# Mamba stage: the output rows' norm statistics from ScalarE sums instead of VectorE bn_stats

## The reference, cut to what matters

```python
x = x + mamba(layernorm(x), ...)      # 16 batches, one after the other
x = x + moe(layernorm(x), ...)        # all 8192 tokens: needs every batch's norm and gate scores
x = x + attention(layernorm(x), ...)
x = x + moe(layernorm(x), ...)

def layernorm(x, eps=1e-05):
    m = mean(x); v = var(x)           # over the 256 channels of a token
    return (x - m) / sqrt(v + eps)
```

## Time and profile before

| what | us |
|---|---|
| median of 3 runs | 3346.77 (3342.35 to 3348.41) |
| span of the profiled execution, first to last instruction | 3323.2 |
| own time of the profiled execution | not given on the page; its span is 23.6 below the median |
| Mamba stage in the profile, start to the last score copy | about 1813 |
| busy over the span: TensorE, VectorE, GpSimd, ScalarE | 2699.6, 2305.5, 2124.3, 1719.1 |

### The profile page before, as it was taken

One profiled execution on the slowest core, in us unless ns is written; L12 is line 12 of the kernel. 1 busy time (PEld: TensorE's weight loads), 2 busy tenths in 40 slices (PEclk: granted clock), 3 DMA queues, 4 the chain that ended last, 5 costly groups with the idle time before them and its releaser, 6 DMA issues.

```text
span 3323.2 us, 54121 instructions
## 1 busy us (share of the span) xinstructions
PE 2699.6 (81%) x20202; PEld 1494.4 (45%) x20202; DVE 2305.5 (69%) x2483; ACT 1719.1 (52%) x3115; POOL 2124.3 (64%) x1317
## 2 busy tenths in 40 slices
PE   5787788877888788887864299996999999269998
PEld 2233333433333334333332156664676777235665
DVE  1799999999999999999996632211666676542211
ACT  3677777777777777777763022222444443022222
POOL 1899999999999999999994035533333333024543
PEclk9899999988998889988976599998999999579999
DMA  3556556665566565665561124432111111213442
GB/s 112 106 128 148 140 140 135 152 142 134 122 147 153 140 141 136 141 147 141 132 130 65 22 58 90 90 58 56 40 46 53 53 46 40 67 34 83 90 90 26
DMA packets 227392, 330.02 MB, mean 99 GB/s; under 512 B 40545, under 2 KB 116833, under 8 KB 227010
## 3 DMA queue, kind: packets, MB, share of 16 engines
q1 hardware_dynamic: 202562, 292.49, 35.8%
q0 software_dynamic: 24576, 34.10, 6.1%
HBM read 240.52 MB, written 85.98 MB: 98 GB/s over the span
## 4 chain that ended last, share of the span: by engine, by line
PE 44%; POOL 25%; DVE 20%; issue 7%; ACT 3%; DMA 2%; SPq 0%; DVEq 0%; POOLq 0%; ACTq 0%
POOL m_side L584 15%; PE t_wb L2062 8%; POOL m_hc L593 7%; DVE m_pair L668 7%; PE f_h L1341 6%; PE g_h L1341 6%; DVE m_hc L668 5%; PE m_wk L771 3%; PE f_yp L1355 3%; PE g_yp L1355 3%; PE t_num L2062 2%; DVE m_hc L677 2%; PE t_a_ps L2062 2%; PE m_y L863 2%; PE m_pair L919 2%
## 5 line engine op out<-in xcount | busy, mean ns | idle before, releaser
L584 POOL TENSOR_TENSOR m_side<-m_du_r,m_bc 128x1024 f32<-128x1024 f32 x416 | 975.0, 2368 | 13.2 <-DMA m_du_r<-ddd 13.0
L351 ACT ACTIVATE m_pair<-m_delta_r,m_a_neg 128x512 f32<-128x512 f32 x832 | 539.7, 681 | 179.1 <-DVE m_hc L677 128.7
L593 POOL TENSOR_TENSOR m_hc<-m_hc,m_bc 128x1024 f32<-128x1024 f32 x208 | 492.3, 2370 | 99.4 <-DVE m_hc L668 97.7
L668 DVE TENSOR_TENSOR_SCAN m_pair<-m_pair,m_side 128x1024 f32<-128x1024 f32 x240 | 548.0, 2283 | 3.3 <-ACT m_pair L351 2.8
L863 PE MATMUL m_y<-m_hc,m_fold 128*32 128x512 f32 x2048 | 322.1, 703 | 229.4 <-DVE m_hc L677 120.9
L668 DVE TENSOR_TENSOR_SCAN m_hc<-m_pair,m_side 128x1024 f32<-128x1024 f32 x176 | 397.8, 2275 | 28.5 <-ACT m_pair L351 28.5
L677 DVE TENSOR_TENSOR m_hc<-m_pair,m_bc 128x1024 f32<-128x1024 f32 x304 | 370.5, 1219 | 7.3
L771 PE MATMUL m_wk<-m_xnT,m_w_in 128*128 128x512 f32 x512 | 276.1, 666 | 10.7 <-DVE m_cw_diag L725 9.8
L771 PE MATMUL m_wk<-m_xs,m_cw_diag 128*128 128x512 f32 x512 | 244.1, 605 | 15.5 <-ACT m_xs L416 15.5
L919 PE MATMUL m_pair<-m_b_diag,m_du_t 128*32 128x128 f32 x6144 | 203.6, 289 | 44.0 <-DVE m_hc L668 24.4
L919 PEld LDWEIGHTS m_pair<-m_b_diag,m_du_t 128*32 128x32 f32 x6144 | 178.8, 117 | 125.1 <-issue 123.7
(11 more groups left out here) (308 smaller groups left out, 4884.8 us busy)
## 6 DMA issues: line engine op xcount, KB each, us to landing
m_delta_r<-ddd SPq DMA_DIRECT2D x256, 256.0 KB, 6.8
m_du_r<-ddd SPq DMA_DIRECT2D x256, 256.0 KB, 7.7
m_bc<-bcd SPq DMA_DIRECT2D x256, 128.0 KB, 3.0
ddd<-m_delta SPq DMA_DIRECT2D x32, 512.0 KB, 3.2
ddd<-m_du SPq DMA_DIRECT2D x32, 512.0 KB, 4.2
f_w<-in_w SPq DMA_DIRECT2D x24, 512.0 KB, 6.2
g_w<-in_w SPq DMA_DIRECT2D x24, 512.0 KB, 6.1
m_xt<-in_x SPq DMA_DIRECT2D x16, 512.0 KB, 10.7
```

Source lines behind the costliest of these rows:

```text
L351: last = nc.scalar.activation(to, delta_r[:, c % 2, q, :], ACT.Exp, scale=a_neg[:, c * NQ + q, st:st + 1])
L584: nc.gpsimd.tensor_tensor(side[:, un % RING, :, :], du_r[:, c % 2, 2 * h:2 * h + 2, :], bc[:, 0, st:st + 1, :].to_broadcast([P, 2, T]), AL ...
L593: nc.gpsimd.tensor_tensor(hc[:, un % RING, :, :], hc[:, un % RING, :, :], bc[:, 1, st:st + 1, :].to_broadcast([P, 2, T]), ALU.mult).then_i ...
L668: nc.vector.tensor_tensor_scan(to, decay, added, 0.0, ALU.mult, ALU.add).then_inc(S["scan"], 1)
```

## The change

VectorE's bn_stats and bn_aggr of the output rows are taken out. ScalarE instead makes two passes over them with an accumulated output: the sum of each row (`out_sums`, function Identity, in units 9 and 12), from it the negated mean (`out_mean`, unit 12), then the sum of the squares of the rows less their mean (`out_squares`, function Square, units 14 and 18). What the passes write besides goes into the tile of the normed rows and is overwritten later. GpSimd's `out_stats` has three operations in place of four and moves from unit 17 to unit 20, the norm `out_norm3` moves from units 20 and 22 to 22 and 23. In the epilogue the same steps follow one another.

```diff
--- before.py
+++ after.py
@@ -171,8 +171,9 @@
 
         xr = s.sb("xr", [P, TJ, C])
         x1t = xr
-        stat1 = s.sb("stat1", [P, TJ, 6])
-        mv1 = s.sb("mv1", [P, TJ, 2])
+        sum1 = s.sb("sum1", [P, TJ])
+        nmean1 = s.sb("nmean1", [P, TJ])
+        sq1 = s.sb("sq1", [P, TJ])
         ve1 = s.sb("ve1", [P, TJ])
         rstd1 = s.sb("rstd1", [P, TJ])
         nm1 = s.sb("nm1", [P, TJ])
@@ -191,7 +192,7 @@
                  "a_exp aneg const one halo diag "
                  "bs agg ve rstd nm xn tr trev ix ixev cv cvev u iz izev sz xp xdev dt "
                  "ab ex sp de du dz "
-                 "btr b_t dut du_t dg0 dg1 dA dBu dBp scan hD hP sum yg op x1 bs1 agg1 ve1 rstd1 nm1 xn1 pt ptev scm scev").split()
+                 "btr b_t dut du_t dg0 dg1 dA dBu dBp scan hD hP sum yg op x1 sum1 agg1 ve1 rstd1 nm1 xn1 pt ptev scm scev").split()
         S = {n: s.sem(n) for n in names}
 
         xv = x.rearrange("b (j p) c -> b p j c", p=P)
@@ -389,6 +390,29 @@
                                                 scale=rstd[:, j:j + 1])
                 if half:
                     last.then_inc(S["xn"], 1)
+
+            def out_sums(b, half):
+                act.wait_ge(S["x1"], b * 2 + half + 1)
+                if half == 0 and not below(b, 1):
+                    act.wait_ge(S["pt"], b * 2)
+                    act.wait_ge(S["st_xn1"], b * 16)
+                    act.wait_ge(S["ve1"], b)
+                for j in range(half * 2, half * 2 + 2):
+                    last = nc.scalar.activation(xn1t[:, j, :], x1t[:, j, :], ACT.Identity, accum_out=sum1[:, j:j + 1])
+                if half:
+                    last.then_inc(S["sum1"], 1)
+
+            def out_mean(b):
+                act.wait_ge(S["sum1"], b * 2 + 1)
+                nc.scalar.activation(nmean1[:], sum1[:], ACT.Copy, scale=-1.0 / C).then_inc(S["sum1"], 1)
+
+            def out_squares(b, half):
+                act.wait_ge(S["sum1"], b * 2 + 2)
+                for j in range(half * 2, half * 2 + 2):
+                    last = nc.scalar.activation(xn1t[:, j, :], x1t[:, j, :], ACT.Square, bias=nmean1[:, j:j + 1],
+                                                accum_out=sq1[:, j:j + 1])
+                if half:
+                    last.then_inc(S["agg1"], 1)
 
             def out_norm3(b, half):
                 act.wait_ge(S["nm1"], b + 1)
@@ -516,8 +540,15 @@
                             silu_u(b + 1, 1 - par)
                         silu_z(b, par)
                         nc.scalar.preload_act_table_set("natural_log_exp_and_others")
-                    if post and un in (20, 22):
-                        out_norm3(b - 1, (20, 22).index(un))
+                    if post:
+                        if un in (9, 12):
+                            out_sums(b - 1, (9, 12).index(un))
+                        if un == 12:
+                            out_mean(b - 1)
+                        if un in (14, 18):
+                            out_squares(b - 1, (14, 18).index(un))
+                        if un in (22, 23):
+                            out_norm3(b - 1, (22, 23).index(un))
                     if prep:
                         if un == 12:
                             xd_out(b + 1)
@@ -548,6 +579,11 @@
                             diag(b + 1, (27, 30, 31, 32, 33, 34, 35, 36).index(un) // NL, (27, 30, 31, 32, 33, 34, 35, 36).index(un) % NL)
 
             def epilogue():
+                for half in range(2):
+                    out_sums(NB - 1, half)
+                out_mean(NB - 1)
+                for half in range(2):
+                    out_squares(NB - 1, half)
                 out_norm3(NB - 1, 0)
                 out_norm3(NB - 1, 1)
                 pt_out(NB - 1, 0)
@@ -571,7 +607,12 @@
                 inv_std(b, mv, ve, rstd, nm, "agg", "ve", "rstd", "nm")
 
             def out_stats(b):
-                inv_std(b, mv1, ve1, rstd1, nm1, "agg1", "ve1", "rstd1", "nm1")
+                wait_alone(pool, S["agg1"], b + 1, S["tick"])
+                nc.gpsimd.tensor_scalar(ve1[:, :], sq1[:, :], 1.0 / C, EPS, ALU.mult, ALU.add).then_inc(S["ve1"], 1)
+                wait_alone(pool, S["ve1"], b + 1, S["tick"])
+                nc.gpsimd.tensor_tensor(rstd1[:, :], ve1[:, :], nhalf[:, :], ALU.pow).then_inc(S["rstd1"], 1)
+                wait_alone(pool, S["rstd1"], b + 1, S["tick"])
+                nc.gpsimd.tensor_tensor(nm1[:, :], nmean1[:, :], rstd1[:, :], ALU.mult).then_inc(S["nm1"], 1)
 
             def times_b(b, un):
                 c, st, h = un // 8, un % 8 // 2, un % 2
@@ -621,7 +662,7 @@
                         times_b(b, un)
                     if un >= 2 and un - 2 in ON_POOL:
                         times_c(b, un - 2)
-                    if post and un == 17:
+                    if post and un == 20:
                         out_stats(b - 1)
                     if ahead(b) and un == 17:
                         in_stats(b + 2)
@@ -694,19 +735,6 @@
                 two = slice(half * 2, half * 2 + 2)
                 nc.vector.tensor_tensor(x1t[:, two, :], wk[:, half, :].rearrange("p (j c) -> p j c", c=C), xr[:, two, :],
                                         ALU.add).then_inc(S["x1"], 1)
-
-            def out_norm1(b, half):
-                dve.wait_ge(S["x1"], b * 2 + half + 1)
-                for j in range(half * 2, half * 2 + 2):
-                    last = nc.vector.bn_stats(stat1[:, j, :], x1t[:, j, :])
-                if half:
-                    last.then_inc(S["bs1"], 1)
-
-            def out_norm2(b):
-                wait_alone(dve, S["bs1"], b + 1, S["tick"])
-                for j in range(TJ):
-                    last = nc.vector.bn_aggr(mv1[:, j, :], stat1[:, j, :])
-                last.then_inc(S["agg1"], 1)
 
             def prologue():
                 nc.vector.memset(xs[:, :, 0:HALO], 0.0).then_inc(S["halo"], 1)
@@ -742,10 +770,6 @@
                             gate(b - 1, 1 - par, 3)
                         if un in (8, 10):
                             residual(b - 1, (8, 10).index(un))
-                        if un in (9, 10):
-                            out_norm1(b - 1, (9, 10).index(un))
-                        if un == 10:
-                            out_norm2(b - 1)
                     if ahead(b):
                         if un in (13, 14):
                             in_norm1(b + 2, 2 * (13, 14).index(un))
@@ -761,8 +785,6 @@
                 gate(NB - 1, (NB - 1) % 2, 3)
                 for half in range(2):
                     residual(NB - 1, half)
-                    out_norm1(NB - 1, half)
-                out_norm2(NB - 1)
 
             batches(prologue, body, epilogue)
```

## The result

| | kernel before | changed kernel |
|---|---|---|
| median of 11 runs each, one chip | 3346.77 us (3342.35 to 3349.24) | 3352.06 us (3349.51 to 3357.46) |
| ratio, 95% interval | | 1.0021 [1.0012, 1.0030] |
| last score copy of the Mamba stage ends, profile | 1813.2 | 1815.9 |

The ratio stands for +7.0 us (4.0 to 10.0), the medians for +5.3. The forecast was +14.0 us and the range 3346 to 3378.

A forecast was written before the change was run, and what follows sets the result against it. VectorE, busy 1356 of 1400 us in the Mamba stage, was taken as the dear engine. 14 batches x 0.95, less 1.4 in the last batch, plus 2.05 in the epilogue gave +14.0 us, 3360.7; range 3346 to 3378.

The forecast's parts named there:

- The tail: Epilogue after the last residual: sums, mean, squares and three GpSimd operations stand before the norm with nothing hidden, +2.05 us.
- the free read: Low end for ScalarE's accumulator read at no cost: two sums take 0.75 us, 0.66 a batch, total +9 us, 3356.
- the second rival: Less TensorE idling keeps its clock, the 1.07 us stall at the delta operation goes, batch even: 3347.4; chance 8%.
- +0.95 us a batch: Unit 9 step: sums delay the convolution copy, output and x projections and exponential 13; scan 13 begins at 671.25, not 670.3.
- Two sums take 1.04 us.: ScalarE's pair of sums: 0.42 us each at 256 columns plus 0.10 per accumulator read, no overlap across the read.
- 0.1 of gap absorbed: TensorE from output to x projection is busy without a gap of note, so the x projection ends 1.18 us later.
- new wait of 0.8 us at scan 13, 14 times: Sign of being right: VectorE waits 0.8 us for ScalarE before scan 13, once in each of 14 batches.
- Rest of the batch: Squares at units 14 and 18, moved norm, GpSimd statistics, later store: nothing, 0.1 us over at most at unit 18.
- Batch 15: Last batch, with no convolution copy and no x projection: VectorE keeps some 1.4 us of its saving.
- The gain comes through: ScalarE's sums hidden, GpSimd's b-products then bound: 1.28 us a batch gained, 3329.5 in all; chance 12%.
- Table switch: Square not in ScalarE's active table set, two loads around each pair: +36 us more, 3397; chance 4%.
- Dear read: Nearly 0.2 us more per accumulator read delays convolution copy and mean: 2.4 a batch, 3381; inside the forecast's 76 points.

The follow-up runs named there:

- vector_saving: Changed kernel without any statistics of the output rows, mean 0 and variance 1 instead, on neither VectorE nor ScalarE; ratio to the kernel before 0.9969.
- sums_at_10: Changed kernel with the first pair of sums moved from unit 9 to unit 10, behind the last convolution copy; ratio to the kernel before 0.9995.
- no_wait_9: Changed kernel with the two sums of unit 9 reading a constant weight tile, so they wait for nothing; ratio to the kernel before 0.9993.
- double_sums2: Changed kernel with two further sums on ScalarE behind the first pair at unit 9; ratio to the kernel before 1.0144.
- half_more: Changed kernel with one further sum on ScalarE behind the first pair at unit 9; ratio to the kernel before 1.0073.

## Why the prediction was right in sign and double in size

**Right.** The mechanism holds, link by link. Starts in the changed kernel with the 2.37 taken off, against those before: convolution copy 658.17 against 657.13, output projection 658.89 against 657.87, second residual 662.65 against 661.62, scan 11 within 0.23, xd copy 668.97 against 668.26, exponential 13 669.45 against 668.74. "All that was removed has been eaten by the wait": vector_saving shows that even the rest would have been worth 0.2 us. sums_at_10 and no_wait_9 show that the wait at unit 9 is the cause. The squares are hidden: they stand with no idle time before them, and no VectorE wait appears behind them. The tail is +1.59 where +2.05 was said. GpSimd never delays VectorE. The time lies in the stated range, but not where the forecast had it: 3352.06 is below the 3356 of its own lower end, and 0.51 a batch below the 0.66 of the free read. The range reached down to 3346 for the sake of the second rival, which did not come; that the time still fell into it is in part luck.

**The term that was mis-sized** is "+0.95 us a batch". Measured: +0.51. Two causes of like size:
- "Two sums take 1.04 us." They take 659.32 - 658.50 = 0.82. The read of the accumulator is busy for 187 ns, but the next instruction starts 0.09 us after it began, and the sum before it is overlapped by 0.09 too. The prediction added the read without overlap. That is 0.22 of the 0.24 by which the copy's +1.28 was too large, measured +1.04. The estimate from the Trainium skill (ScalarE: Activation LUTs, What ACT_TABLE_LOAD costs) for a free read was 0.71; the 0.82 of the trace lies between it and the 1.04, nearer to the estimate.
- "0.1 of gap absorbed" between the output and the x projection. From start to start these lay 664.55 - 657.87 = 6.68 apart, now 667.62 - 661.26 = 6.36: 0.32 absorbed, most of it in a gap that stood before TensorE's second total.

So exponential 13 came +0.71 and not +1.18, and of this its old slack of 0.2 is taken off. The "new wait of 0.8 us at scan 13, 14 times" is 0.15 us each time: scan 12 ends at 670.72 + 2.28 = 673.00, exponential 13 at 671.82 + 1.30 = 673.12, scan 13 starts at 673.15. The 0.8 us in 5 stalls in the list above are those of these waits that just pass its limit of 0.15. So a good part of the delay had come with VectorE itself, from the second residual: scan 12 starts 0.23 later than before (668.35 against 668.12).

**Rest of the batch.** "Nothing" was wrong by -0.29 to -0.03 a batch, in favour. In one batch the same four matmuls of the input projection took 3.78 us before and 1.98 after the change:

```profile
711.48 3.78 PE L771 MATMUL m_wk<-m_xnT,m_w_in 128*128 128x512 f32 x4
```

```profile
713.50 1.98 PE L793 MATMUL m_wk<-m_xnT,m_w_in 128*128 128x512 f32 x4
```

The granted clock there was 0.50 and 1.00. This is what the second rival (the delta wait) describes, but at another place: the delta wait itself stayed in 13 of 14 batches. That such phases of the clock make the whole difference was argued, not tested.

**Batch 15**: -1.4 said, -2.5 to -2.7 measured. With no convolution copy and no x projection all of VectorE's 1.9 us came through: the last output projection starts 77.18 us after the batch's first residual (1717.34) instead of 79.13 (1713.72), 1.95 us sooner. The rest, 0.54, is TensorE's, whose last output projection ran at a higher granted clock, 0.79 instead of 0.74. Before, then changed kernel:

```profile
1792.85 9.63 PE L771 MATMUL m_wk<-m_w_out,m_yg 128*128 128x256 f32 x32 [0.80 <-DVE m_yg L688]
```

```profile
1794.52 9.09 PE L793 MATMUL m_wk<-m_w_out,m_yg 128*128 128x256 f32 x32 [0.80 <-DVE m_yg L729]
```

**The sum.** With the measured terms the sum is 14 x 0.51 - 2.6 + 1.6 = +6.1, less 0.4 to 4 from the rest of the batches; the medians gave +5.3 and +5.2, the ratios +7.0 and +4.4.

**The rivals.** *The gain comes through* fell, and its bound too: in sums_at_10 not GpSimd's lead but exponential 13 behind the xd copy held VectorE, and no order tried won more than 0.8 us to the gate or 0.3 a batch. *The delta wait absorbs the delay* fell: that wait stayed. *Table switch* fell: no load was added. *Dear read* was the opposite of what came. A rival that was missing is the one that double_sums2 and half_more found: a delay larger by 0.4 us lets the clock fall under the output projection in 6 of 14 batches, one larger by 0.8 in 13.

## What to carry to other kernels

A pass moved onto an engine with a quarter of slack is priced at the first thing it waits for and by what is queued behind it: here 0.82 us of work delayed the second residual by 1.04 at unit 9 and by nothing one unit later. Before time is taken off the busiest engine, remove it without putting it anywhere: here 1.9 us a batch were worth 0.3, and no version of the move tried here won more over a batch. Work that is hidden in a loop stands bare in the epilogue, and may stay on the old engine there.

## What was not expected of the hardware

- ScalarE's read of an accumulator shows 187 ns of busy time but takes 0.09 us of the queue: sums start 0.42 us apart.
- TensorE's clock fell with a little more idling in front: after 1.80 us of idling 16 matmuls took 3.72 us, after 2.20 either 3.72 or 5.41, after 2.60 always 5.41, but once after 2.79 they took 3.72. A delay of 0.8 us so cost 2.4.
- Chips seem to differ where this kernel's Mamba stage does not. The kernel before ran in 3324.8 us on one chip and in 3346.3 and 3346.6 on two others. Behind the Mamba stage lie 1511 to 1515 us in the four profiles from the first of these chips and 1532 to 1535 in those from the other two. The two profiles of before differ in the same way: 1510.0 and 1531.7 us behind the stage, and from the first to the last matmul with the weights of the first MoE 350.4 and 360.9, with the Mamba stage ending at 1813.2 and 1814.1.
